# A gated cross-attention and expert layer on one core: block 4's GpSimd parts behind the context's low parts, and block 5's norm and turn inside a second layer

## The chip, the cores and the metric

The kernel runs on one core of a Trainium2 chip (trn2). The metric is the device time of one execution in microseconds; the median of three runs counts. Engines are called TensorE (PE in the profile), VectorE (DVE), ScalarE (ACT), GpSimd (POOL) and SyncE (SP). SyncE only issues DMA transfers here.

## The reference

The input x has 16 sequences of 256 rows of 256 numbers, the context 16 sequences of 120 rows. Cut to what matters:

```python
# cross part: z is the context, x the normalized input
z  = z @ W_in + b_in
zn = layernorm(z)
h  = silu(pe @ Wp1 + bp1) @ Wp2 + bp2            # taps, times a decaying window
c  = (causal convolution of zn with window * h, every second row)
xr = ffn(x)                                      # layernorm, W1a, silu, W1b, + x
y  = ffn(xr * c)                                 # layernorm, W2a, silu, W2b, + x
x  = x + tanh(g_xattn) * y
# expert part: 8 heads of 32 numbers, 16 experts, the best 2 of each row and head
t  = (layernorm(x) @ Wm + bm), rows and heads as rows
w  = softmax(t @ expert_emb), top 2
out = sum over the two of w * (gelu(t @ W1[e] + b1[e]) @ W2[e] + b2[e])
x  = x + tanh(g_ffn) * (out @ Wo + bo)
```

## The kernel before, in words

The 4096 rows of x are 8 blocks of 512 rows. Each engine has its program written out by hand, in one order, and waits on semaphores that count finished steps. Numbers that need more precision than 16 bits are split in a high and a low 16-bit part, and a product is three matmuls: high by high, high by low, low by high.

The first stage goes over the blocks with s = 1 to 8. For block s, TensorE does the second layer of block s-1 (`layer2`, L650: bias, then 4 quarters k of 12 products) and the first layer of block s (`layer1`, L633), with the input turned by TensorE (`turn`, L604, eight transposes) from the normalized block. The norm itself is VectorE's: `first_norm(b)` takes the statistics (L973, L980, L1012, L1013), GpSimd raises to the power -1/2 (`power`, L1713), and `normed_twice(b)` writes the normalized rows (L990; on ScalarE for blocks 3 and 4). ScalarE writes the high part of the turned input (L1523), VectorE the low part (`turn_lo`, L956). After the first layer ScalarE writes the activation twice, as a high part and in full (L1529, L1534), and GpSimd subtracts the two for the low part (`layer1_lo`, L1719). `first_out(b)` on VectorE (L1155) ends the block.

The context is normalized in pieces in the gaps (`context_part`, L1118, L1121). At s = 4 ScalarE copies its high parts (`context_hi`, L1618) and VectorE subtracts the low parts (`context_lo`, L1131) in five pieces; semaphore `v_zl` counts them.

The convolution has 32 chunks of 8 channels. A chunk is 32 small matmuls (`conv`, L676), ScalarE's copy of the sums (`conv_sums`, L1546), TensorE's turn back (`flip`, L696, four or so transposes, one chunk behind) and VectorE's addition (`conv_out`, L1139), counted by `v_dc`; `flip(c)` waits for the output of chunk c-2. Chunks 0 to 7 follow the first layer of block 4, 8 to 15 that of block 5, 16 to 23 that of block 6, and 24 to 31 come at s = 7. So blocks 5, 6 and 7 are turned inside the convolution, ahead of chunks 6, 14 and 22 (`turn_ahead`), into PSUM banks that nothing else uses then.

The taps of a chunk (four DMA transfers of 134 KB, `load_T`, L386) go in a ring of ten places. SyncE issues those of chunk c+10 or so when chunk c is done. Its queue also holds the swaps of the context's halves (`swap_context`, L441) and the loads of x (`load_x`, L374): block 7's x goes to the place of block 5's, so it waits for block 5's norm (`v_nm` at 6). When the convolution is done, the gating, the second feed-forward layer and the expert part follow; nothing of them is changed.

ScalarE splits the weights of the later stages at s = 5 (L1514, L1516), and VectorE takes their low parts then (L940).

Of the kernel before, what the change touches and what calls it, by code (L numbers as in the profile page):

```python
# [13 lines left out]
NB = 8  # L14
NC = 32
# [50 lines left out]
def turn3(b):  # L66
    return norm3(b)
# [15 lines left out]

def turn_ahead(c):

    return c // 8 + 5 if c % 8 == 6 and c < NC - 8 else None


AGAIN = (4, 5, 6, 8, 9, 0, 1, 2)
# [55 lines left out]
def flamingo_kernel(nc, xd, ctxT, peT, wp1, wp2, win, w1a, w1b, w2a, w2b, wm, wo,  # L145
                    ew1, ew2, eb, cols, rows, ident, ramp, tvec, ones, out):
    with ExitStack() as ctx:
# [11 lines left out]
        W1 = {h: sb("W1" + h, 2048, F16) for h in "hl"}  # L159
# [210 lines left out]
        def sync_program(sp):  # L370
# [73 lines left out]
            for s in range(1, NB + 1):  # L444
                if s in (2, 4):
                    sp.wait_ge(v_nm, s + 1)
                    load_x(0, 5 if s == 2 else 6)
                if s == 4:
                    swap_context(0)
                    swap_context(1)  # L450
                for c in chunks(s):
                    for e in next_in_place(c):
                        load_T(e)
                    if c < 3:
                        swap_context(c + 2)
                    if c == 3:
                        sp.wait_ge(v_nm, 6)
                        load_x(0, 7)
                if s == NB - 1:
                    for b in range(2):  # L460
                        sp.wait_ge(v_nm, 8 - b)
                        load_x(1, b)
# [75 lines left out]
        def tensor_program(pe):  # L538
# [98 lines left out]
            def layer2(j, w, halfway=None):  # L637

                o = [PB[:, 256 * t:256 * t + 256] for t in range(4)]
                bias = BR[:, 256 * (j // NB):256 * (j // NB) + 256].unsqueeze(1).broadcast_to([128, 2, 256])  # L640
                for h in range(2):
                    pe.matmul(PB[:, 512 * h:512 * h + 512].rearrange("p (t n) -> p t n", t=2), ON[:, 0:128], bias,
                              start=True, stop=False)
                for k in range(4):
                    if k == 2 and halfway:
                        halfway()
                    pe.wait_ge(g_slo, 4 * j + k + 1)
                    for t in range(4):
                        for a, b in THREE:
                            m = pe.matmul(o[t], S[b][:, 512 * k + 128 * t:512 * k + 128 * t + 128],  # L650
                                          w[a][:, 1024 + 256 * k:1024 + 256 * k + 256],
                                          start=False, stop=(k == 3 and t % 2 == 1 and a + b == THREE[2]))
                m.then_inc(p_l2, 1)
# [59 lines left out]
            def first_gated():  # L713
                gated_turn(0)

            def third_turn(b):
                pe.wait_ge(*((a_n3, b + 1) if b < 7 else (v_n3, 1)))
                turn(turn3(b), WSP[:, 1024 * b:1024 * b + 1024])
# [52 lines left out]
            for s in range(1, NB + 1):  # L771
                if s < 5:
                    first_turn(s)
                if s == 3:
                    pe.wait_ge(l_w2, 80)
                    pe.wait_ge(a_silu, 11)
                    affine_bias(1, PA[:, 1024:1152])
                if chunks(s - 1):
                    pe.wait_ge(v_dc, UPTO[s - 1] - 1)
                if s == 1:  # L780
                    pe.wait_ge(v_w1l, 3)
                    pe.wait_ge(v_tap, 2)
                    pe.wait_ge(g_br, 1)
                    pe.wait_ge(g_one, 1)
                else:
                    pe.wait_ge(v_out, s - 1)
                layer2(s - 1, W1, first_gated if s == NB else None)
                if s == 7:
                    convs(s)
                if s < NB:  # L790
                    layer1(s, s, W1)
                if s < 7:
                    convs(s)
# [143 lines left out]
        def vector_program(ve):  # L937
# [77 lines left out]
            def normed_twice(b):  # L1015
                o = 160 + 48 * (b % 3)
                ve.wait_ge(g_pow, b + 1)
                if b == 2:
                    ve.wait_ge(g_br, 1)
                apply(x_place(b)[0], XN0[b % 3], SM[:, o + 24:o + 32], SM[:, o + 36:o + 40], v_nm)  # L1020
# [8 lines left out]
            def once_over_twice(b):  # L1029

                o = 160 + 48 * (b % 3)
                ve.reciprocal(SM[:, o + 40:o + 44], SM[:, o + 36:o + 40]).then_inc(v_rc, 1)
                ve.wait_ge(v_rc, b + 1)
                ve.scalar_tensor_tensor(out=SM[:, o + 40:o + 44], in0=SM[:, o + 40:o + 44], scalar=SC,
                                        in1=SM[:, o + 32:o + 36], op0=ALU.mult, op1=ALU.mult).then_inc(v_rho, 1)
# [284 lines left out]
            once_over_twice(2)  # L1320
            first_norm(3)
            for s in range(2, NB):
                if s < 5:
                    turn_lo(s)
                if s == 3:
                    layer1_bias(1, PA[:, 1024:1152])
                if s < 5:
                    context_part(*CTX[s][0])
                if s < 4:
                    twice_shift(s + 1)  # L1330
                    once_over_twice(s + 1)
                elif 4 < s < NB - 1:
                    normed_twice(s + 1)
                    once_over_twice(s + 1)
                if s < 5:
                    context_part(*CTX[s][1])
                if s == 5:
                    ve.wait_ge(a_wm, 1)
                    split_lo(WMS, WM["h"][:, :], WM["l"][:, :], v_wm)
                    ve.wait_ge(a_wo, 1)  # L1340
                    split_lo(WOS, WO["h"][:, :], WO["l"][:, :], v_wo)
                    for i, (c0, c1, scale) in enumerate(((0, 512, G2S[0]), (512, 1024, G2S[1]), (1024, 2048, SC))):
                        ve.wait_ge(a_w2h, i + 1)
                        split_lo(XR[:, 4096 + c0:4096 + c1], W2["h"][:, c0:c1], W2["l"][:, c0:c1], v_w2l, scale)
                if s == 6:
                    ve.wait_ge(a_eb, 1)
                    split_lo(EBF, EB["h"][:, :], EB["l"][:, :], v_eb)
                if s == 4:
                    context_lo(0)
                first_out(s - 1)  # L1350
                if s == 4:
                    for u in range(1, 5):
                        context_lo(u)
                elif s + 2 < NB:
                    first_norm(s + 2)
                if s < 5:
                    context_part(*CTX[s][2])
                for c in chunks(s):
                    if c % 8:
                        conv_out(c - 1)  # L1360
                    if turn_ahead(c):
                        turn_lo(turn_ahead(c))
                    if c == 2:
                        normed_twice(5)
                        once_over_twice(5)
                    if c == 4:
                        first_norm(6)
                    if last(c):
                        conv_out(c)
            gate(0)  # L1370
# [139 lines left out]
        def scalar_program(ac):  # L1510
# [121 lines left out]
                        layer1_full(s, C_B1A, 3)  # L1632

            for s in range(1, NB):
                if s < 5:
                    turn(s)
                if s in (2, 3):
                    normed_twice(s + 1)
                if s == 5:
                    ac.wait_ge(l_w2, 80)  # L1640
                    split_hi(WMS, WM["h"][:, :], a_wm)
                    split_hi(WOS, WO["h"][:, :], a_wo)
                    for k in range(2):
                        split_hi(XR[:, 4096 + 512 * k:4608 + 512 * k], W2["h"][:, 512 * k:512 * k + 512], a_w2h, G2S[k])
                    split_hi(XR[:, 5120:6144], W2["h"][:, 1024:2048], a_w2h)
                if s == 6:
                    split_hi(EBF, EB["h"][:, :], a_eb)
                if s == 7:
                    convs_summed(s)
                if s == 4:  # L1650
                    for u in range(3):
                        context_hi(u)
                    for n in range(2):
                        layer1(s, C_B1A, (n,))
                        context_hi(n + 3)
                else:
                    layer1(s, C_B1A, range(3 if s in (5, 6) else 4))
                if s < 7:
                    convs_summed(s)
# [48 lines left out]
        def pool_program(po_):  # L1708
# [35 lines left out]
            po_.wait_ge(v_zep, 1)  # L1744
            po_.tensor_tensor(zr, zr, SM[:, 6:7].broadcast_to([128, 16]), ALU.pow).then_inc(g_zpow, 1)
            for s in range(1, NB - 1):
                layer1_lo(s)
                if s + 2 < NB:
                    power(s + 2)
# [123 lines left out]
```

## Time and profile before

| what | value |
|---|---|
| median of 3 runs | 797.74 us (796.12 to 798.57) |
| the profiled execution | 796.66 us |
| its span, first to last instruction | 794.9 us |
| mean granted TensorE clock | 0.998 |
| TensorE busy | 765.6 us, 96% |
| VectorE busy | 564.6 us, 71% |
| ScalarE busy | 662.9 us, 83% |
| GpSimd busy | 506.2 us, 64% |

The profile is of one execution. A stage is read from the rows of its own stretch, since the shares are means over stages that differ. "issue" as a releaser is time in which an engine waited for nothing that the profile shows. The DMA share is a mean over the core's 16 DMA engines and can come out somewhat over 1. A clock of 1 is 2.4 GHz, of 0.5 it is 1.2 GHz.

### The profile page before, as it was taken

To read this page: it belongs to the slowest core of one execution; us is meant where nothing else is said; L and a number is where in the kernel's file an instruction comes from. 1 tells how busy PE (TensorE), PEld (TensorE's weight loads), DVE (VectorE), ACT (ScalarE), POOL (GpSimd) and SP (SyncE) were. 2 spreads that over 40 slices of the span, in tenths; PEclk is the share of its full clock that TensorE was granted. 3 is DMA by queue.
4 is the path that set the end of the run, shared out by engine and by line. 5 is a ranking of instruction groups with operands and counts; after the bars stand their busy time and mean duration, and the time that the engine had idled before them with its cause. 6 is when DMAs were issued, how large, how long until landed. Compare 5 with 4: busy or idle time off the path is not lost.

```text
span 794.9 us, 23935 instructions
## 1 busy us (share of the span) xinstructions
PE 765.6 (96%) x9972; PEld 384.9 (48%) x9972; DVE 564.6 (71%) x1031; ACT 662.9 (83%) x837; POOL 506.2 (64%) x389
## 2 busy tenths in 40 slices
PE   9999789889899999999999999999999999999997
PEld 4667456655576664333344444444444434444433
DVE  5998963478788995675776776776776776775445
ACT  4464844367778867799999999999999999999995
POOL 1365331047764452587788788787797787797674
PEclk9999999999999999999999999999999999999999
DMA  8994599930123325757455555655555565555542
GB/s 292 222 234 91 127 198 196 204 91 27 34 77 91 75 66 141 173 150 191 140 162 153 162 150 160 170 148 162 159 158 157 154 171 150 158 163 152 168 148 68
DMA packets 86122, 117.07 MB, mean 147 GB/s; under 512 B 13154, under 2 KB 65746, under 8 KB 85915
## 3 DMA queue, kind: packets, MB, share of 16 engines
q1 hardware_dynamic: 86014, 115.55, 55.8%
q8 instruction: 78, 1.28, 0.7%
q14 instruction: 30, 0.24, 0.1%
HBM read 101.28 MB, written 6.94 MB: 136 GB/s over the span
## 4 chain that ended last, share of the span: by engine, by line
PE 76%; DVE 11%; ACT 6%; issue 4%; POOL 3%; POOLq 0%; DVEq 0%; ACTq 0%
PE PB L851 26%; PE PA L839 18%; PE PT L839 9%; PE PB L650 5%; PE PA L633 5%; PE PB L873 2%; DVE WK L956 2%; PE PA L585 2%; ACT WK L1694 2%; DVE SM L973 2%; ACT WK L1559 1%; POOL WK L1719 1%; PE PT L731 1%; DVE DC L1139 1%; PE PB L696 1%
## 5 line engine op out<-in xcount | busy, mean ns | idle before, releaser
L1786 POOL TENSOR_TENSOR WK<-WK 128x512 f32<-128x512 f32 x238 | 330.5, 1389 | 94.4 <-DVE WK L1418 83.9
L1694 ACT ACTIVATE WK<-PA 128x1024 f32<-128x1024 f32 x349 | 354.9, 1112 | 7.5 <-PE PA L839 7.5
L851 PE MATMUL PB<-WK,EW 128*32 128x512 f32 x2040 | 264.8, 593 | 0.3 <-DVE WK L1418 0.3
L839 PE MATMUL PA<-RA,EW 98*32 98x512 f16 x2800 | 200.7, 378 | 1.6 <-ACT WK L1694 1.6
L1694 ACT ACTIVATE WK<-PT 128x1024 f32<-128x1024 f32 x163 | 182.2, 1118 | 0.1
L1719 POOL TENSOR_TENSOR WK<-WK 128x512 f16<-128x512 f32 x64 | 83.5, 1316 | 124.0 <-ACT WK L1534 123.0
L839 PEld LDWEIGHTS PA<-RA,EW 98*32 98x32 f16 x2800 | 71.7, 95 | 149.6 <-issue 78.7
L839 PE MATMUL PT<-RA,EW 98*32 98x512 f16 (+1 forms) x1312 | 99.5, 378 | 0.3 <-ACT WK L1694 0.2
L851 PEld LDWEIGHTS PB<-WK,EW 128*32 128x32 f32 x2040 | 63.4, 111 | 50.7 <-DVE WK L1418 1.1
L1418 DVE SCALAR_TENSOR_TENSOR WK<-PB,CV,W2h 128x512 f32<-128x512 f32 x64 | 48.1, 751 | 42.0 <-PE PB L851 41.4
L1418 DVE SCALAR_TENSOR_TENSOR WK<-PB,CV,DC 128x512 f32<-128x512 f32 x64 | 48.1, 751 | 38.2 <-PE PB L851 37.3
L1418 DVE SCALAR_TENSOR_TENSOR WK<-PB,CV,W1h 128x512 f32<-128x512 f32 x64 | 48.0, 751 | 32.5 <-PE PB L851 29.2
L839 PEld LDWEIGHTS PT<-RA,EW 98*32 98x32 f16 x1312 | 34.3, 95 | 69.4 <-issue 37.2
L1418 DVE SCALAR_TENSOR_TENSOR WK<-PB,CV,W2l 128x512 f32<-128x512 f32 x63 | 47.3, 751 | 26.6 <-PE PB L851 25.7
L1529 ACT ACTIVATE WK<-PA,CV 128x512 f16<-128x512 f32 x64 | 44.2, 691 | 24.6 <-PE PA L633 24.0
L1713 POOL TENSOR_TENSOR SM<-SM 128x4 f32<-128x4 f32 (+1 forms) x24 | 33.2, 1385 | 39.7 <-DVE SM L986 22.7
L650 PE MATMUL PB<-W2h,WK 128*128 128x256 f16 x256 | 42.6, 273 | 4.5 <-POOL WK L1719 4.5
L1534 ACT ACTIVATE WK<-PA,CV 128x512 f32<-128x512 f32 x64 | 44.3, 692 | 0.0
L650 PE MATMUL PB<-W1h,WK 128*128 128x256 f16 x256 | 42.4, 273 | 0.0
L633 PE MATMUL PA<-WK,W1h 128*128 128x512 f16 x128 | 38.1, 379 | 0.0
L633 PE MATMUL PA<-WK,W2h 128*128 128x512 f16 x128 | 38.1, 379 | 0.0
L650 PE MATMUL PB<-W2l,WK 128*128 128x256 f16 x128 | 34.9, 273 | 0.0
(238 smaller groups left out, 1090.9 us busy)
## 6 DMA issues: line engine op xcount, KB each, us to landing
W1h<-wtd SPq DMA_DIRECT2D x128, 128.0 KB, 2.7
DC<-wtd SPq DMA_DIRECT2D x128, 128.0 KB, 2.8
W2h<-wtd SPq DMA_DIRECT2D x128, 128.0 KB, 2.8
W2l<-wtd SPq DMA_DIRECT2D x128, 128.0 KB, 2.8
RA<-wpd SPq DMA_DIRECT2D x96, 134.1 KB, 5.7
WK<-in_x SPq DMA_DIRECT2D x15, 512.0 KB, 4.1
RA<-DC SPq DMA_DIRECT2D x96, 64.0 KB, 2.0
out<-WK SPq DMA_DIRECT2D x16, 256.0 KB, 2.8
```

What stands on the lines that cost most here:

```text
L585: a = pe.matmul(PA[64 * r:64 * r + 64, 512 * q0 + 256 * b:512 * q0 + 256 * b + 256], DC[:, 2048 * k + 128 * bb + 64 * r:2048 * k + 128 * b ...
L633: m = pe.matmul(pa, w[a][:, 512 * k + 128 * n:512 * k + 128 * n + 128], xt[b][:, 512 * k:512 * k + 512], start=(i == 0), stop=(i == 5))
L650: m = pe.matmul(o[t], S[b][:, 512 * k + 128 * t:512 * k + 128 * t + 128], w[a][:, 1024 + 256 * k:1024 + 256 * k + 256], start=False, stop= ...
L839: m = pe.matmul(pre(k)[32 * j:32 * j + 32, w * q:w * q + w], EW1[0:98, 128 * e + 32 * j:128 * e + 32 * j + 32], TS[0:98, h, t0:t0 + w], st ...
L851: m = pe.matmul(o[32 * q:32 * q + 32, :], EW2[:, 32 * e:32 * e + 32], hb[:, 512 * q:512 * q + 512], start=True, stop=True)
L1418: ve.scalar_tensor_tensor(out=dst, in0=po("down", n), scalar=col(C_B2 + e), in1=WB[n // 2 % 4][:, 512 * (n % 2):512 * (n % 2) + 512], op0= ...
L1529: ac.activation(S["h"][:, 512 * n:512 * n + 512], PA[:, 512 * n:512 * n + 512], ACT.Silu, scale=1.0 / SC, bias=col(bcol + n))
L1534: ac.activation(SF[n], PA[:, 512 * n:512 * n + 512], ACT.Silu, scale=1.0 / SC, bias=col(bcol + n)).then_inc(a_silu, 1)
L1694: ac.activation(HB[n % NH][:, 1024 * p:1024 * p + 1024], pre(k)[:, :], ACT.Gelu, scale=1.0 / (SC * SC)).then_inc(a_gelu, 1)
L1713: po_.tensor_tensor(SM[:, o:o + n], SM[:, o:o + n], SM[:, 6:7].broadcast_to([128, n]), ALU.pow).then_inc(g_pow, 1)
L1719: po_.tensor_tensor(sl, SF[n], sh, ALU.subtract).then_inc(g_slo, 1)
L1786: po_.tensor_tensor(AC[g], AC[g], PR[m % 3], ALU.add).then_inc(g_ac, 1)
```

## The change

Four things are moved. GpSimd's four parts of block 4's first layer now wait until all five low parts of the context are done. VectorE's `normed_twice` and `once_over_twice` of block 5 and `first_norm` of block 6, which stood in the convolution's chunks 2 and 4, come after chunk 7, with the low part of block 5's turn behind them; `normed_twice` and `once_over_twice` of block 6 move behind the output of block 4. Block 5's turn leaves the convolution (chunk 6) and stands between the second and the third quarter of block 4's second layer on TensorE, and before the weight splits on ScalarE. SyncE's load of block 7's x moves from chunk 3 to chunk 5.

```diff
--- before.py
+++ after.py
@@ -83,7 +83,7 @@
 
 def turn_ahead(c):
 
-    return c // 8 + 5 if c % 8 == 6 and c < NC - 8 else None
+    return c // 8 + 5 if c in (14, 22) else None
 
 
 AGAIN = (4, 5, 6, 8, 9, 0, 1, 2)
@@ -453,7 +453,7 @@
                         load_T(e)
                     if c < 3:
                         swap_context(c + 2)
-                    if c == 3:
+                    if c == 5:
                         sp.wait_ge(v_nm, 6)
                         load_x(0, 7)
                 if s == NB - 1:
@@ -712,6 +712,9 @@
 
             def first_gated():
                 gated_turn(0)
+
+            def fifth_turn():
+                first_turn(5)
 
             def third_turn(b):
                 pe.wait_ge(*((a_n3, b + 1) if b < 7 else (v_n3, 1)))
@@ -784,7 +787,7 @@
                     pe.wait_ge(g_one, 1)
                 else:
                     pe.wait_ge(v_out, s - 1)
-                layer2(s - 1, W1, first_gated if s == NB else None)
+                layer2(s - 1, W1, {5: fifth_turn, NB: first_gated}.get(s))
                 if s == 7:
                     convs(s)
                 if s < NB:
@@ -1320,7 +1323,11 @@
             once_over_twice(2)
             first_norm(3)
             for s in range(2, NB):
-                if s < 5:
+                if s == 5:
+                    normed_twice(5)
+                    once_over_twice(5)
+                    first_norm(6)
+                if s < 6:
                     turn_lo(s)
                 if s == 3:
                     layer1_bias(1, PA[:, 1024:1152])
@@ -1329,9 +1336,9 @@
                 if s < 4:
                     twice_shift(s + 1)
                     once_over_twice(s + 1)
-                elif 4 < s < NB - 1:
-                    normed_twice(s + 1)
-                    once_over_twice(s + 1)
+                elif s == 6:
+                    normed_twice(7)
+                    once_over_twice(7)
                 if s < 5:
                     context_part(*CTX[s][1])
                 if s == 5:
@@ -1352,6 +1359,9 @@
                     for u in range(1, 5):
                         context_lo(u)
                 elif s + 2 < NB:
+                    if s == 5:
+                        normed_twice(6)
+                        once_over_twice(6)
                     first_norm(s + 2)
                 if s < 5:
                     context_part(*CTX[s][2])
@@ -1360,11 +1370,6 @@
                         conv_out(c - 1)
                     if turn_ahead(c):
                         turn_lo(turn_ahead(c))
-                    if c == 2:
-                        normed_twice(5)
-                        once_over_twice(5)
-                    if c == 4:
-                        first_norm(6)
                     if last(c):
                         conv_out(c)
             gate(0)
@@ -1632,7 +1637,7 @@
                         layer1_full(s, C_B1A, 3)
 
             for s in range(1, NB):
-                if s < 5:
+                if s < 6:
                     turn(s)
                 if s in (2, 3):
                     normed_twice(s + 1)
@@ -1744,6 +1749,8 @@
             po_.wait_ge(v_zep, 1)
             po_.tensor_tensor(zr, zr, SM[:, 6:7].broadcast_to([128, 16]), ALU.pow).then_inc(g_zpow, 1)
             for s in range(1, NB - 1):
+                if s == 4:
+                    po_.wait_ge(v_zl, 5)
                 layer1_lo(s)
                 if s + 2 < NB:
                     power(s + 2)
```

## Rows read from the trace of the kernel before

**Rows 1.** The page: the profiled span.

```profile
span 794.9 us, 23935 instructions
```

**Rows 2.** Windows: busy us of PE, PEld, DVE, ACT, POOL; clock; DMA; GB/s.

```profile
118.60:122.80 4.20, 4.15 (x76) 3.08 (x75) 0.69 (x1) 1.79 (x3) 0.00 (x0) 0.60 1.11 192
104.00:158.00 54.00, 46.83 (x845) 31.59 (x843) 23.63 (x51) 22.59 (x40) 10.87 (x9) 0.97 1.11 201
```

**Rows 3.** The chain that ended last: start us, us, what.

```profile
98.42 0.61 PE PB L642 x2
...
104.27 5.18 PE PA L633 x24
...
115.10 3.56 issue
...
142.73 0.87 issue
...
161.51 1.24 issue
```

**Rows 4.** Timeline of DVE: start us, us, engine, line, operation, out<-in [idle before <-releaser].

```profile
82.35 6.02 DVE L1131 TENSOR_TENSOR RA<-DC,RA 128x512 f16<-128x512 f32 x4
...
89.68 2.22 DVE L990 TENSOR_SCALAR WK<-WK,SM 128x256 f32<-128x256 f32 x4
...
94.72 0.38 DVE L980 BATCH_NORM_AGGREGATE SM<-SM 128x2 f32<-128x6 f32 x4
...
98.87 1.38 DVE L990 TENSOR_SCALAR RA<-WK,SM 128x256 f32<-128x256 f32 x4
...
102.98 1.22 DVE L940 SCALAR_TENSOR_TENSOR W2l<-XR,W2h 128x1024 f16<-128x1024 f32 x1
...
106.36 1.41 DVE L973 BATCH_NORM_STATS2 SM<-WK 128x6 f32<-128x256 f32 x4 [0.30 <-DMA WK<-in_x]
```

**Rows 5.** Line L1131, 78 to 90 us: duration ns min/median/max, starts, forms.

```profile
L1131 DVE TENSOR_TENSOR RA<-DC,RA x5: 685/1214/2180, 80.2 to 87.2; 128x1024 f16<-128x1024 f32 x3, 128x512 f16<-128x512 f32 x2
```

**Rows 6.** Timeline of PE, 89 to 114 us.

```profile
89.22 0.66 PE L696 MATMUL PB<-ID,RMP 128*128 128x128 f32 x4 [0.45 <-DVE DC L1139]
...
92.84 0.66 PE L696 MATMUL PB<-ID,RMP 128*128 128x128 f32 x4 [1.25 <-DVE DC L1139]
93.33 1.04 PE L604 MATMUL PA<-ID,WK 128*128 128x128 f32 x8
...
113.09 0.65 PE L696 MATMUL PB<-ID,RMP 128*128 128x128 f32 x4
```

**Rows 7.** Timeline of POOL: the first and the last of four.

```profile
82.84 1.21 POOL L1719 TENSOR_TENSOR WK<-WK 128x512 f16<-128x512 f32 x1 [7.02 <-ACT WK L1534]
...
90.14 1.28 POOL L1719 TENSOR_TENSOR WK<-WK 128x512 f16<-128x512 f32 x1 [0.76 <-ACT WK L1534]
```

**Rows 8.** Timeline of ACT: the first and the last of the weight splits.

```profile
96.64 0.62 ACT L1514 ACTIVATE WMh<-WK 128x512 f16<-128x512 f32 x1
...
98.90 1.05 ACT L1514 ACTIVATE W2h<-XR 128x1024 f16<-128x1024 f32 x1
```

**Rows 9.** Timeline of SP's DMA issues.

```profile
98.89 2.69 SPq L386 DMA_DIRECT2D RA<-wpd  x4
101.63 0.42 SPq L374 DMA_DIRECT2D WK<-in_x  x1
102.09 6.69 SPq L386 DMA_DIRECT2D RA<-wpd  x12
```

**Rows 10.** Landing us of the x load issued at 101.63; the page's DMA issues.

```profile
DMA to landing us min/median/max: 4.7/4.7/4.7
...
XR<-in_w1b SPq DMA_DIRECT2D x1, 512.0 KB, 11.4
```

**Rows 11.** DMA queues, 99.8 to 115.6, 115.6 to 118: packets, MB, share.

```profile
q1 hardware_dynamic: 5292, 3.15, 101.8%
...
q8 instruction: 1, 0.02, 3.4%
```

## The prediction

> **What bounds the kernel now.** I read the page first, then the chain of work that ended last, then each engine's timeline from 80 to 126 us, where the edits lie. The profiled execution took 796.66 us for a span of 794.9 [rows 1], 1.8 outside it; the median of the three runs is 797.74, so I make the sum on the profile and add 1.1. The edits touch only what lies between 80 and 166 us, the end of the convolution, so a gain has to come from there and survive to 166.
>
> In that stretch three things set the pace. Up to 98.4 it is VectorE: its low parts of the context, one group of 6.02 us [rows 4], and then a norm of 2.22 us and the statistics, with TensorE waiting 0.45 and 1.25 us for a convolution output [rows 6]. From 98.42 TensorE runs the second layer of block 4 (to 104.27, 5.85 us with its wait) and the first layer of block 5 without a pause [rows 3]. From 104 to 158 the DMA engines are full, at a share of 1.11 and 201 GB/s [rows 2], with tap loads. There the chain has three pauses called "issue", of 3.56, 0.87 and 1.24 us [rows 3]. They wait for no semaphore. Over 99.8 to 115.6 us, 5292 packets of the data queue moved and none of an instruction queue; in the next 2.4 us one packet of the instruction queue came [rows 11], and TensorE went on at 118.65, the end of the 3.56 us pause. So I read them as TensorE out of code, because its next block of instructions stood behind full data queues. After that pause the granted clock is 0.60 over 118.6 to 122.8 [rows 2], which is mostly the lower of the two levels, 1.2 GHz, and costs 4.2 x 0.4 = 1.7 us.
>
> **GpSimd waits for the context's low parts.** Five VectorE subtractions of 0.69 (small) or 1.21 (large) us took up to 2.18 when a GpSimd part of 1.21 us ran beside them [rows 5, 7]. Two are slowed, so 2 x 0.97 = 1.9 us leave the group of 6.02; the last one cannot begin before ScalarE's high part, so I count 1.3. The Trainium skill (SBUF — State Buffer, Who interferes with whom) says a VectorE instruction with two SBUF inputs blocks against a GpSimd one that reads SBUF, and a reduction never does; the trace agrees on the first by 2.18 against 1.21. GpSimd's four parts of some 1.3 us each then end near 92.3 instead of 91.4 [rows 7]; layer 2 of block 4 needs them after 94.8, so that costs nothing. If the cover went, the price would be at most that 0.9.
>
> **The norms and the turn leave the convolution of block 4.** Out of it go, on VectorE, the norm (2.22, of which 0.84 is contention, since its twin takes 1.38 [rows 4]), its reciprocal, the statistics (1.4 plus 0.6 of small ones) and the turn's low part (1.3); on TensorE, the turn, 1.04 [rows 6]. TensorE then goes at the pace of a convolution and a flip, 1.15 us a chunk (my estimate: from the flip at 113.09 [rows 6] to the pause at 115.10 [rows 3], in which lie two flips, one convolution and the first instruction of chunk 13, are 2.0 us, so 1.7 without that instruction for one and a half chunks). The flip at 89.22 loses its wait of 0.45 and comes near 88.7; from there this gives chunk 7 at 92.75, its flip at 94.1, and layer 2 of block 4 at 94.8: 3.6 us earlier than 98.42.
>
> Inside layer 2 the turn comes after the bias and half the products, some 3.1 of its 5.85 us, at 97.9. It needs block 5's norm: VectorE finishes the last two outputs at 95.4, and 1.38 more is 96.8. One microsecond to spare, so no wait; a norm slowed once by GpSimd (0.84) still fits. The turn puts 1.0 us back, and layer 1 of block 5 begins at 94.8 + 5.85 + 1.0 = 101.6, 2.6 us before 104.27. Its operand's low part is done at 100.5. ScalarE does its high part by 99.6 (my estimate: the end of the turn at 98.9 and half a microsecond) and only then the weight splits, which took from 96.64 to 99.95, 3.3 us [rows 8]: to 102.9, just when layer 1 asks for its first activation (101.6 and a quarter of its 5.18 us). Free, with nothing to spare. VectorE's own splits follow ScalarE's and end with one of 1.22 [rows 4], at 104.3, so the output of block 4 ends at 106.0, much as before. The convolution of block 5 would begin at 106.8 instead of 109.4.
>
> **What is late next: the last x block.** VectorE now does the norm of block 6 after that output (1.4, or up to 3.1 if GpSimd hits two of its four pieces), to 107.4 to 109.1, and then wants the statistics of block 7. On SyncE's queue the load of that x moves from behind chunk 3's tap load to behind chunk 5's, past eight DMA issues, and gains a wait for block 5's norm (96.8, long fulfilled). Queued behind it are the tap loads of chunks 16 on, wanted at 137, so nobody feels them. The load went out at 101.63 and landed 4.7 us later [rows 9, 10], at 106.3, when VectorE had waited 0.30 for it [rows 4]. Twelve issues take 6.69 us [rows 9], so eight take some 4: it goes out at 105.5 to 106.1. Below, with the same 4.7 us, it lands at 110.2. Above, by bytes: two tap loads of four DMAs of 134 KB are 1.07 MB now ahead of it, at 201 GB/s 5.4 us, so 111.7. I take 111.7, because the DMA engines are full. Then statistics 2.0, output of chunk 8 0.7: 114.4. The flip of chunk 10, which waits for that output and was at 113.09 [rows 6], comes at 114.5: TensorE stands idle 4 us (113.09 - 2.6 = 110.5, to 114.5). The convolution of chunk 13 follows 1.7 later, at 116.2. Before, it got its first instruction in and then the rest at 118.65, the end of the pause. Its code block is asked for some 2.6 us sooner and should be there by about 115.5. So the pause of 3.56 is replaced by this wait of 4, the lower clock after it stays, and the gain at this point is 118.65 - 116.2 = 2.4 us.
>
> **How much of it is left at 166.** TensorE now asks for each later block 2.4 us sooner, but the data queues empty no sooner: the DMA engines are busy to 158 with the same bytes [rows 2]. Two code pauses lie ahead, at 142.7 and 161.5 [rows 3]. If a block comes after all the data queued before it, TensorE gets it at the old hour; if its delay is fixed, it moves with the request. I take the middle, half kept: 1.2 us. Sum: 796.66 - 1.2 = 795.5 on the profile, 796.6 beside the median. From -0.3 to +0.3% is about what a measurement of this kernel cannot tell from no change; that is 2.4 us. The convolution's end is followed by VectorE's gate and then fixed work, so what is left at 166 is left at the end.
>
> The skill has two rules on this. Runtime: NRT & Kernel Launch (Instruction fetch mechanics) holds that refills are mostly hidden; the trace disagrees, by the 3.56 us pause; were it so, chunk 13 would not have paused before, and the wait for x would make the change 1.4 us slower there (114.5 against 113.09). DMA: Bandwidth & Descriptors (Queues, rings and completion order) says each DMA engine goes round its queues packet by packet; then a block's delay would not hang on the depth of the data queue, and the sum would be the "kept" rival's.
>
> **Rivals.**
> - Code blocks fully bound to the data stream: TensorE comes to the pause before 161.5 earlier and leaves it at the same 162.75. Gain 0: 797.7. For it: the DMA share of 1.11 that stays to 158. Against: the later pauses are short.
> - Kept: the delay moves with the request, all 2.4 us stay: 795.3. For it: the two later pauses are no longer than 1.24, though the queues are as full. Against: the pause of 3.56.
> - More than that: x lands at 110.2, or the 4 us idle does not lower the clock (1.7 us back). Then 2.4 + 1.5 or + 1.7, about 4.0: 793.7. Against: 3.56 us of idle did lower it.
> - Slower: the x load comes late. The longest landing of a 512 KB load is 11.4 us [rows 10]; from 105.5 it would be at 116.9, chunk 13 at 121.4, later than 118.65 by 2.8: 800.5. It decides from a landing past 114.1 (loss), and past 116.5 for 0.3%. Against: that one stood behind a row of large loads.
> - The change does nothing where it is put: the turn halfway waits for the norm and gives back the 2.6. It needs VectorE 1.1 us late before it costs anything, and 3.7 to cost all; it ends at 797.7 too, and I count it with the first rival.
>
> **Chances.** Forecast (half kept) 0.38; bound to the stream 0.22; kept 0.15; more 0.14; slower 0.11. Faster by over 0.3%: 0.14 and two thirds of the kept case (it lies on the border), 0.24. Slower: 0.11. Within: 0.65. The range has to reach both sides: 793.7 leaves out the far half of the "more" case, 799.3 nearly all of the slower one. The forecast's own range is 795.3 to 797.7.
>
> **What would show it.** No VectorE low part over 1.25 us; layer 2 of block 4 at 94.8 and layer 1 of block 5 at 101.6; a turn between its products without a wait; the wait of VectorE for x up from 0.3 to 2.5 to 4 us; a TensorE wait of 4 us for VectorE ahead of chunk 10's flip, and no "issue" pause at chunk 13; then "issue" pauses before chunks 21 and 29 longer than 0.87 and 1.24 by one to two microseconds together. It is wrong if the x load lands by 109, if chunk 13 still pauses for code, if the clock stays at 2.4 GHz, or if ScalarE's splits make layer 1's first activation late.

## The result, and the profile after

The changed kernel takes 798.87 us (median of 22 runs, 797.45 to 800.93), the kernel before 797.31 (22 runs, 792.28 to 801.47). The ratio is 1.0025, with a 95% interval of 1.0013 to 1.0037: slower by 0.25%, some 2 us (1.6 us between the medians): clear of the noise, though small. The forecast was 796.6, faster by 0.15%. The profiled execution of the changed kernel took 800.92 us, which is the slow end of its runs; a second profile, of an execution of 798.82, is read beside it below.

The chain of work that ended last, in the changed kernel (start us, us, what; SPq is SyncE's queue of DMA issues):

```profile
101.70 0.43 SPq L386
...
104.74 0.67 SPq L386
105.41 0.04 issue
105.45 9.34 DMA WK<-in_x
114.79 0.02 issue
114.81 1.42 DVE SM L976 x4
...
116.91 0.60 DVE DC L1142
117.51 0.04 issue
117.55 1.11 PE PB L696 x4
...
149.38 0.60 PE PB L642 x2
...
161.48 2.53 issue
164.01 0.90 PE PA L696 x3
...
169.87 0.70 DVE DC L1142
```

The same chain in the kernel before, where the last pause of [rows 3] lies between its two rows:

```profile
149.40 0.61 PE PB L642 x2
...
166.49 0.70 DVE DC L1139
```

The timelines of TensorE and VectorE in the changed kernel:

```profile
94.43 0.60 PE L642 MATMUL PB<-BR,ON 128*128 128x512 f16 x2
97.49 1.04 PE L604 MATMUL PA<-ID,WK 128*128 128x128 f32 x8
100.98 0.59 PE L633 MATMUL PA<-WK,W1h 128*128 128x512 f16 x2
...
109.41 0.63 PE L676 MATMUL PA<-RA 60*32 60x256 f16 x32
117.55 0.69 PE L696 MATMUL PB<-ID,RMP 128*128 128x128 f32 x2 [7.52 <-DVE DC L1142]
...
120.62 1.05 PE L676 MATMUL PA<-RA 60*32 60x256 f16 x32
```

```profile
105.48 2.88 DVE L993 TENSOR_SCALAR RA<-WK,SM 128x256 f32<-128x256 f32 x4
...
114.81 1.41 DVE L976 BATCH_NORM_STATS2 SM<-WK 128x6 f32<-128x256 f32 x4 [6.16 <-DMA WK<-in_x]
```

The same kernel in windows; the columns are those of [rows 2]:

```profile
112.00:122.20 10.20, 4.65 (x75) 2.93 (x76) 4.60 (x14) 1.04 (x2) 1.63 (x1) 0.50 1.12 185
163.20:170.00 6.80, 5.99 (x80) 3.84 (x81) 2.21 (x4) 1.19 (x2) 0.00 (x0) 0.50 0.16 30
```

And the kernel before behind its last pause:

```profile
161.50:168.00 6.50, 5.03 (x88) 3.12 (x88) 3.12 (x5) 1.83 (x4) 0.00 (x0) 1.00 0.28 78
```

What is to be seen. Up to the convolution of block 5 the change does what it was to do: layer 2 of block 4 starts at 94.43 instead of 98.42, and layer 1 of block 5 at 100.98. Then the chain no longer runs through TensorE but through SyncE's queue: the x load of block 7 goes out at 105.45, behind the tap loads, and lands 9.34 us later. VectorE waits 6.16 us for it where it waited 0.30 [rows 4], and TensorE waits 7.52 us for VectorE's output, longer than the 3.56 us pause for code that is gone [rows 3]. The clock is at its lower level from 112.0, inside that wait, to 122.2; TensorE is busy for 4.65 of these 10.2 us. The convolution of chunk 13, which had its first instruction at 114.82 and the others at 118.65 before, starts at 120.62, and layer 2 of block 5 at 127.15 instead of 126.04. Even so layer 2 of block 6 starts at 149.38, as in the kernel before (149.40 in its chain): the pause of 0.87 us at 142.7 is gone too. The loss comes behind it. The last pause begins at the same time as before (161.48, before 161.51) but grows from 1.24 to 2.53 us, and the clock falls at its end, at 163.2, for 6.8 us, in which TensorE is busy for 5.99. The last output of the convolution starts at 169.87 instead of 166.49.

The clock is not a matter of one profile: the 22 executions of the changed kernel had a mean granted clock of 0.988 to 0.994 (median 0.991), 99 executions of the kernel before, on the chips of the experiments, 0.990 to 1.000 (median 0.996). Half a per cent of the time is 4 us of full speed; part of it fell into waits, so the 4 us are an upper estimate of its price.

### The profile page after: what moved, and what is told of

Its sections match the earlier page's. It is cut to its first block, busy times and chain, and to the rows that moved or that the text cites. A ratio compares the mean times of both kernels' runs of the same rounds, so it can differ in the third digit from the quotient of the medians.

```text
span 799.1 us, 23936 instructions
## 1 busy us (share of the span) xinstructions
PE 767.9 (96%) x9972; PEld 395.0 (49%) x9972; DVE 563.1 (70%) x1031; ACT 662.8 (83%) x837; POOL 506.2 (63%) x389
## 3 DMA queue, kind: packets, MB, share of 16 engines
q8 instruction: 78, 1.28, 0.7%
## 4 chain that ended last, share of the span: by engine, by line
PE 72%; DVE 9%; ACT 7%; SPq 4%; issue 3%; POOL 3%; DMA 2%; POOLq 0%; DVEq 0%; ACTq 0%
PE PB L854 26%; PE PA L842 18%; PE PT L842 9%; PE PB L650 4%; PE PA L633 4%; PE PB L876 2%; PE PA L585 2%; SPq L386 2%; DVE WK L959 2%; ACT WK L1699 2%; DVE SM L976 2%; ACT WK L1564 1%; DMA WK<-in_x 1%; POOL WK L1724 1%; ACT WK L1539 1%
## 5 line engine op out<-in xcount | busy, mean ns | idle before, releaser
L842 PEld LDWEIGHTS PA<-RA,EW 98*32 98x32 f16 x2800 | 75.3, 95 | 146.2 <-issue 75.0
L854 PEld LDWEIGHTS PB<-WK,EW 128*32 128x32 f32 x2040 | 66.6, 111 | 48.3 <-DVE WK L1423 1.9
L842 PEld LDWEIGHTS PT<-RA,EW 98*32 98x32 f16 x1312 | 36.0, 95 | 67.8 <-issue 35.5
```

The source lines that it names most:

```text
L842: m = pe.matmul(pre(k)[32 * j:32 * j + 32, w * q:w * q + w], EW1[0:98, 128 * e + 32 * j:128 * e + 32 * j + 32], TS[0:98, h, t0:t0 + w], st ...
L854: m = pe.matmul(o[32 * q:32 * q + 32, :], EW2[:, 32 * e:32 * e + 32], hb[:, 512 * q:512 * q + 512], start=True, stop=True)
```

## The experiments

All ratios are against the kernel before, run on the same chip, with 95% intervals; the chips differ from one group of experiments to the next. A profile is of one execution, and executions of one kernel differ by up to 10 us, so times from two profiles are weaker evidence than the ratios. In every profile of the study, the span less the start of the last convolution output is 628.3 to 629.2 us, so the difference between kernels lies nearly all ahead of that output.

**The x load back behind chunk 3** (in the changed kernel):

```diff
-                    if c == 5:
+                    if c == 3:
                         sp.wait_ge(v_nm, 6)
                         load_x(0, 7)
```

> The changed kernel, with SyncE's load of block 7's x back behind chunk 3's tap load. Theory (the moved load is what costs): the load goes out at 101.2 us and lands near 106, VectorE waits at most 1 us for it, TensorE's wait of 7.8 us before the flip of chunk 10 falls to 1 to 1.5 us, the granted clock does not fall at 112, and the kernel is 2 to 5 us faster than the changed one: 794 to 797. Rival (the moved load only fills a pause that would come anyway, TensorE waits for code instead): a pause of 3 us or more marked issue comes near chunk 13, and the time stays within 1 us of the changed kernel, near 799.

Measured: 795.04 us, 0.9972 [0.9945, 0.9999]; the changed kernel's ratio is 1.0025. The load landed after 5.2 us, VectorE did not wait for it, and TensorE's wait fell to 1.28. TensorE in that kernel:

```profile
109.72 0.63 PE L676 MATMUL PA<-RA 60*32 60x256 f16 x32
111.63 0.66 PE L696 MATMUL PB<-ID,RMP 128*128 128x128 f32 x4 [1.28 <-DVE DC L1142]
...
113.36 0.28 PE L676 MATMUL PA<-RA 60*32 60x256 f16 x1
114.94 0.30 PE L676 MATMUL PA<-RA 60*32 60x256 f16 x8 [1.30 <-issue]
```

The theory holds: the load's new place costs the kernel some 0.5%, more than the whole loss, and with the load in its old place the rest of the change gains about what was forecast. The last pause did not go: it is 2.64 us in this profile, again with a low clock behind it. The profiled execution (797.25 us) is one of the slower ones of this kernel; its executions took 790.47 us (mean clock 1.000) to 799.57 us (0.993), so the pauses do not come in all of them at this length.

**Only the x load moved** (in the kernel before, the reverse edit alone).

> The kernel before, with only that load moved from behind chunk 3's to behind chunk 5's tap load. Theory (the load's hour alone costs): it goes out near 105.5 and lands near 115, VectorE waits 8 us for it, the flip of chunk 10 comes near 117.5 instead of 113.1, and the kernel is 1.5 to 4 us slower than before. Rival (the loss comes from the moved norms and turn): at most 0.5 us slower, because the pause for code at chunk 13 covers it.

Measured: 797.97 us, 1.0008 [0.9993, 1.0024]. Landing 7.3 us, VectorE's wait 6.44, but TensorE's only 2.08, for here it is ready for the flip some 2.5 us later than in the changed kernel, and no pause for code at chunk 13 follows. The theory's 1.5 to 4 us did not come. So the rival holds for this edit alone: the late load is covered by a stall that was there. It seems to cost only where the other edits have brought TensorE forward.

The two kernels side by side show where a lead ends. First the x load alone, then the changed kernel with the load behind chunk 3 (end of block 6's chunks, the last pause, the last output):

```profile
148.73 0.61 DVE DC L1139
...
165.14 0.70 DVE DC L1139
```

```profile
146.92 0.61 DVE DC L1142
...
159.68 2.64 issue
...
167.00 0.70 DVE DC L1142
```

The second is 1.8 us ahead at chunk 23 and 1.9 us behind at chunk 31. It reaches the border of its code block early, waits 2.64 us, and then runs at 1.2 GHz:

```profile
163.80:167.20 3.40, 3.40 (x44) 2.19 (x43) 1.59 (x3) 0.90 (x2) 0.00 (x0) 0.50 0.29 65
```

The first comes late, finds its block there and keeps its clock from chunk 23 on (it had lost it before, for 3.4 us from 142.2, at a pause of 1.62).

**The second layer's x loads behind the convolution.** SyncE issues two loads of 512 KB at 152 to 155 us, ahead of TensorE's last code block. In this edit they are issued after `p_conv` has counted all chunks:

```diff
-                if s == NB - 1:
-                    for b in range(2):
-                        sp.wait_ge(v_nm, 8 - b)
-                        load_x(1, b)
             sp.wait_ge(p_conv, NC)
             sp.dma_start(ES[0:98, :], ew1).then_inc(l_ew, 16)
+            for b in range(2):
+                sp.wait_ge(v_nm, 8 - b)
+                load_x(1, b)
```

In the changed kernel:

> The changed kernel, with the two loads of x for the second layer (SyncE, at 152 us in the kernel before) moved behind the end of the convolution. Theory (TensorE's code blocks come only when the data issued before them has drained, and the last pause of the convolution is set by these 1 MB): the pause of 2.5 us at 161.5 and the low clock after it are gone or under 1.5 us, the convolution ends near 166 instead of 169.9, and the kernel is 2 to 4 us faster than the changed one: 795 to 797. Rival (the pause is of another kind, or the block's delay is fixed): pause and time as in the changed kernel, 799.

In the kernel before:

> The kernel before with the same two loads moved behind the end of the convolution. Theory: the pause of 1.24 us at 161.5 shrinks to under 0.5 us, 0.8 to 2 us faster than before: 795.5 to 796.7. The pause at chunk 13 (3.56 us) stays, since those loads come later. Rival: no change, 797.5; or slower, because the second layer now waits for x.

Measured: 794.10 us, 0.9972 [0.9949, 0.9995], and 794.20 us, 0.9956 [0.9936, 0.9975]. In both profiles the last pause is gone, and the clock is at 2.4 GHz from 121.1 us on at the latest. The changed kernel with this edit, from chunk 23 to 31:

```profile
146.71 0.61 DVE DC L1141
...
162.99 0.70 DVE DC L1141
```

16.3 us where the changed kernel took 21.1 (148.72 to 169.87), although its own wait for the x of block 7 is still there (TensorE 4.02 us). Both gains are above or at the upper end of what was expected (the second was to be 0.8 to 2 us; it is 2.5 us between the medians and 3.5 by the ratio). The executions say where it comes from: the kernel before took 791.93 to 800.96 us on that chip, with the edit 791.74 to 795.74. The fastest are no faster; the slow ones are gone. So in many executions the pause with its clock seems to cost the kernel before more than in the profiled one.

The instruction queue shows the block itself. Its packet lies in the half microsecond from 160.0 in the kernel before, from 161.5 in the changed one, and from 156.5 and 155.5 in the same two with the x loads moved (packets, MB, share of the 16 engines):

```profile
q8 instruction: 1, 0.02, 14.0%
q8 instruction: 1, 0.02, 13.8%
q8 instruction: 1, 0.02, 17.8%
q8 instruction: 1, 0.02, 12.7%
```

| us | x loads issued | border before the last passed | packet of the last block | TensorE past the border | pause |
|---|---|---|---|---|---|
| before | 152.3 | 157.3 | 160.4 | 162.8 | 1.24 |
| only the x load of block 7 moved | 151.9 | 157.3 | 159.0 | 161.4 | none |
| changed | 155.3 | 157.3 | 161.6 | 164.0 | 2.53 |
| changed, x behind chunk 3 | 153.3 | 155.5 | 159.8 | 162.3 | 2.64 |
| before, x loads behind the convolution | 162.8 | 156.1 | 156.6 | 160.0 | none |
| changed, x loads behind the convolution | 162.0 | 155.3 | 155.8 | 159.2 | none |

In all thirteen profiles a pause for code from 108 us on ends 2.4 to 3.1 us after its packet, so the packet sets its end. In the nine with the x loads in front, that packet comes between 159.0 and 161.6, whether TensorE passed the border before it at 155.1 or at 157.3, and it is latest (161.6) where these loads were issued latest (155.3). In the two versions without them it comes 0.5 us after that border is passed.

**Code blocks shifted.** In the kernel before, 48 small matmuls stand at TensorE's start, 96 records, into a bank that is overwritten before use.

```diff
             pe.wait_ge(g_one, 1)
+            for _ in range(48):
+                pe.matmul(PT[0:32, 0:32], ON[:, 0:32], ON[:, 0:32], start=True, stop=True)
             ones(6)
```

> The kernel before with 48 matmuls of 32 columns more at TensorE's start, 96 instruction records, written to a bank that is overwritten before use. Theory (the pauses marked issue stand at the borders of code blocks of 256 instructions): each of the pauses at the records 2240, 3008 and 3777 comes 96 records of the old program earlier, so the one at chunk 13 moves to about chunk 11 or 12 and the one of chunk 29 to chunk 27 or 28, and the old places run through. The time is within 1.5 us of before plus up to 2 us for the matmuls. Rival (the pauses belong to those instructions, or to a moment of the data stream): they stay at the same chunks.

Measured: 796.03 us, 0.9994 [0.9970, 1.0019]. The profiled execution is the slowest of its twelve (802.38). The windows count TensorE's records from the start to the begin of each long pause. The kernel before, then the shifted one:

```profile
0.00:115.10 115.10, 108.65 (x1095) 67.64 (x1096) 95.99 (x261) 65.90 (x106) 48.14 (x42) 1.00 0.83 194
0.00:142.70 142.70, 131.51 (x1469) 83.08 (x1470) 105.86 (x282) 76.74 (x125) 52.83 (x46) 0.99 0.88 194
0.00:161.50 161.50, 148.26 (x1843) 95.45 (x1843) 114.60 (x296) 82.63 (x136) 52.83 (x46) 0.99 0.90 195
```

```profile
0.00:119.20 119.20, 112.17 (x1221) 71.36 (x1222) 96.93 (x262) 67.90 (x110) 48.09 (x42) 1.00 0.85 193
0.00:145.10 145.10, 134.97 (x1595) 86.53 (x1595) 106.94 (x284) 78.86 (x129) 52.72 (x46) 0.99 0.89 192
0.00:159.20 159.20, 147.24 (x1844) 95.49 (x1845) 113.58 (x295) 81.85 (x134) 52.72 (x46) 0.99 0.91 191
```

Matmuls and weight loads together are 2191, 2939 and 3686 before, and 2443, 3190 and 3689 shifted. With TensorE's semaphore instructions, which the trace has and the windows leave out, the counts are 2241, 3009 and 3777, and 2497, 3265 and 3777: all apart by multiples of 256. The shifted program has a shorter pause of 0.61 us at 113.60 too, behind record 2241. In all thirteen profiles every "issue" pause of 0.6 us or more between 108 us and the convolution's end stands behind record 2241, 2497, 3009, 3265 or 3777. So the pauses sit at fixed counts of the instruction stream and not at a chunk: the theory holds. The expectation that all three come 96 records earlier in the program was right for the last and, as the 0.61 us, for the first; two long ones stand one block further on, for which borders pause depends on when TensorE gets there and when the packet comes. The shifted program's last pause is 4.72 us, the longest of the study.

The Trainium skill (Runtime: NRT & Kernel Launch, Instruction fetch mechanics) gives refills of 256 instructions; the trace agrees, by these counts. It also says the cost of a border is mostly hidden; the trace agrees for six of the seven borders that the changed kernel's profile passes between 110 and 165 us, and not for the ones with pauses of 2.5 to 4.7 us.

**Both corrections together** (the changed kernel, x of block 7 behind chunk 3, the second layer's x behind the convolution).

> The changed kernel with block 7's x load back behind chunk 3 and the two x loads of the second layer behind the end of the convolution. Theory: both prices of the change are gone: no wait of VectorE for x over 1 us, no pause over 1.5 us at the last code block and no low clock after it; the convolution ends near 163.5 and the kernel takes 791 to 793.5, faster than both. Rival (something else holds the end of the convolution): 795, as with the first of the two edits alone.

Measured: 792.04 us, 0.9939 [0.9919, 0.9959]: faster than both kernels, by 0.6% than the one before. The convolution's last outputs start at 160.49, better than the 163.5 expected, and what bounds it in this profile is a tap load at last:

```profile
152.29 5.92 DMA RA<-wpd
158.22 0.14 issue
158.35 1.05 PE PA L675 x27
```

Most of the lead of this profile was there before the moved loads' turn came: chunk 23's output starts at 141.42, against 146.92 with the first correction alone, and the pause behind record 3009 is 0.34 us instead of 2.17. The second correction changes nothing ahead of it, so that part belongs to the execution; for the kernels, the ratios count.

**GpSimd's wait.** Alone in the kernel before, and taken out of the changed kernel:

```diff
             for s in range(1, NB - 1):
+                if s == 4:
+                    po_.wait_ge(v_zl, 5)
                 layer1_lo(s)
```

> The kernel before with only GpSimd's wait for the context's five low parts. Theory: no low part over 1.25 us, the norm of block 5 at 1.4 to 3.1 us (GpSimd now runs beside it), layer 2 of block 4 at most 1.3 us earlier, and nothing left of it at the end of the convolution: within 1 us of before. Rival: all 1.3 us stay, 796.

> The changed kernel without GpSimd's wait. Theory: layer 2 of block 4 begins 1.3 us later than in the changed kernel (95.9 instead of 94.6), the x load still goes out near 105.5 and lands near 115, so nothing changes behind it: within 1 us of the changed kernel, near 799. Rival (GpSimd's wait itself costs, by parts that come late): 1 us or more faster than the changed kernel.

Measured: 796.47 us, 0.9995 [0.9977, 1.0014], and 797.65 us, 1.0009 [0.9993, 1.0025]. Then out of the two corrected versions:

> The changed kernel with block 7's x load back behind chunk 3 and without GpSimd's wait: only the norms and the turn are moved. Theory (the norms and the turn give the gain, GpSimd's wait adds at most 1.3 us at the start of layer 2 of block 4, which the code pauses swallow): as with the load moved back and the wait in place, 0.997 of before within 0.15%. Rival (GpSimd's wait gives a good part of the gain): 0.999 to 1.000 of before.

> The fastest version so far (block 7's x load behind chunk 3, the second layer's two x loads behind the convolution) without GpSimd's wait. Theory: its end of the convolution is bound by the tap load of chunk 31, so the wait is worth nothing there: 0.994 of before within 0.15%. Rival: the wait's 1.3 us count in full, 0.9955.

Measured: 795.93 us, 0.9990 [0.9967, 1.0012] (0.9972 with the wait), and 793.36 us, 0.9946 [0.9927, 0.9965] (0.9939 with it). The four comparisons differ in sign, none is over 0.2%, and their intervals overlap; which way the wait works stays open. Not all came as expected. With the wait alone, layer 2 of block 4 began at 99.42, not earlier than 98.42. The changed kernel without it was to take some 799 us with x landing near 115; it took 797.65, with a landing at 111.9. The version with x behind chunk 3 was to be within 0.15% of 0.997 without the wait; 0.9990 fits the rival, that the wait gives a good part of the gain. The last version hit its number, but in its profile no tap load bounds the end, which comes at 158.03. The wait does shorten the low parts (at most 1.23 us with it, 2.18 without); a gain from that at the end is not shown.

**The changed kernel once more.**

> The changed kernel once more, for a second profile. Theory (the x load lands 7.2 to 9.3 us after its issue, as in four profiles with the moved load): TensorE waits 3.5 to 8 us before the flip of chunk 10, at least one pause for code or a low clock is gone or new against the first profile, and the time is 0 to 0.4% above the kernel before. Rival (the landing of 9.3 us belongs to that one execution): 7.2 to 7.6 again, a wait under 4.5 us, and the time as with the moved load and without GpSimd's wait, within 0.1% of before.

Measured: 797.61 us, 1.0013 [0.9994, 1.0033], as the theory had it. The load landed after 8.6 us, at 112.5, TensorE waited 4.52, chunk 13 started at 118.34, and both low stretches are there again:

```profile
113.90:120.70 6.80, 5.43 (x79) 3.71 (x80) 3.45 (x12) 1.19 (x2) 1.64 (x1) 0.50 1.12 188
161.70:168.50 6.80, 5.95 (x80) 3.84 (x81) 2.18 (x4) 1.19 (x2) 0.00 (x0) 0.50 0.14 31
```

So the second stretch does not hang on the 7.52 us wait of the first profile. TensorE comes to the last border at 159.57, 1.9 us before the kernel before, and pauses 2.97 us; it leaves at 162.54, 0.2 before it. The last output starts at 168.40, 1.9 us behind it.

## Why the prediction was wrong, point by point

**What failed first: the lead at chunk 13.** The sum had the x load landing at 111.7, the flip of chunk 10 at 114.5, and chunk 13 at 116.2, 2.4 us ahead of 118.65. It landed at 114.8, the flip came at 117.55 and chunk 13 at 120.62, 2.0 behind; in the second profile at 112.5, 115.27 and 118.34, 0.3 ahead. Of the 4.4 us in the first profile, 3.1 are the landing. The other 1.4 are the clock: the prediction kept the low clock but took 1.7 us from the flip to chunk 13 from rows at full clock, while the clock fell inside the wait and that way took 3.07 us in both profiles.

The landing was 106.3 plus 5.4, from 1.07 MB at 201 GB/s. The issue at 105.45 was right in the first profile (105.5 to 106.1 was forecast) and came at 103.9 to 104.7 in the four others with the load behind chunk 5. There the landing takes 7.2 to 9.3 us; with the load behind chunk 3 it takes 4.7 to 7.1 in eight profiles, so the 4.7 it was built on is the shortest of a spread. What shares the rate with the load was not settled. TensorE waited 7.52 and 4.52 us, not 4.0. The prediction's slower rival named this mechanism and its point ("past 114.1") but gave it 0.11. Undoing it is worth 0.5%: with the load behind chunk 3 the ratio is 0.9972. It is still not the whole loss in the first profile, for at 149.38 the changed kernel was level with the one before.

**What failed next: how much of a lead is left at 166.** The prediction took "the middle, half kept: 1.2 us", between keeping all and keeping nothing, as if a TensorE that comes early to a code border could only wait there until "the old hour". The runs show a third answer, below the lower bound: the pause can end later than before, and the clock falls in it. In the second profile a lead of 1.9 us at the last border left 0.2 behind it. In the first there was no lead at that border, and the block itself came 1.2 us later (161.6 against 160.4), as the x loads in front of it had been issued 3.0 us later. The last pause was 2.53 and 2.97 us in the two profiles, against 1.24, and in it the granted clock fell to 0.50 for 6.8 us, where the kernel before kept 1.00. 5.95 to 5.99 us of busy time at half clock is some 3 us of work lost. The experiments isolate it: with nothing but the 1 MB of x loads taken from in front of the last code block, both the pause and the low clock go, and the ratio of the changed kernel falls from 1.0025 to 0.9972. That the clock falls because of the longer pause is argued, from the order in the profiles: in all six with a last pause of 2.5 us or more a low stretch begins in it or behind it, and in the six with 1.24, 0.38 or none there is none. The combined version had a pause of 0.51 there and several short waits for tap loads, and its clock fell at 157.1 for 3.4 us, so a single long pause is not the only way to it; and at chunk 13 a pause of 2.55 us left the clock at 1.00 in the kernel before with the x loads moved, so it is not a sure one either.

**What held.** The largest low part took 1.23 us (no more than 1.25 was forecast). Layer 2 of block 4 came at 94.43 (94.8), layer 1 of block 5 at 100.98 (101.6), the turn inside the second layer at 97.49 (97.9) without a wait. The norm of block 6, hit by GpSimd, took 2.88 us (1.4 to 3.1), hidden by the wait for x. The pause for code at chunk 13 was replaced by the wait for VectorE; its block's packet came at 111.2 and 112.0 in the two profiles instead of 115.7, in time as forecast. The low clock stayed, but with 4.65 us of busy time in it instead of 3.4. "Pauses longer before chunks 21 and 29" was half right: the one at 142.7 went, the other grew by 1.3.

**The rivals.** "Bound to the data stream" was the right mechanism at the last border, as read from [rows 11], with the wrong floor. The Trainium skill (DMA: Bandwidth & Descriptors, Queues, rings and completion order) has the engines go round their queues packet by packet; from this the "kept" rival had all of the lead stay. The last block's packet does not bear it out: it came 1.7 to 6.2 us after TensorE passed the border before, in the nine profiles with the x loads in front, where one data packet took 0.06 to 0.07 us, and 0.5 to 2.4 us after it in the four without them. How the engines chose between the queues was not tested.

## What to carry to other kernels

A pause marked "issue" on an engine with a long unrolled program is a late code block when its count of records from the start stays fixed while the program shifts under it. Data issued ahead of it on full DMA queues made it late here, so a large load that nobody needs yet is worth holding back until the engine has crossed the next border; that was worth 0.44% here, where the change with its x load in the old place gave 0.28% at its best. And a lead won ahead of such a border is not a gain: ask how long the engine will stand there and whether the clock falls, and when a load is moved past others on a full queue, price it by the longest landing seen in that stretch, not by its bytes or by the landing of one profile.

## What the runs showed of the hardware

The load of block 7's x, 512 KB, took 4.7 to 9.3 us to land, depending on place and execution, with the DMA engines at a share of 1.1. TensorE's pauses without a releaser stood behind records 2241, 2497, 3009, 3265 and 3777 of its stream, 256 or a multiple apart, and ended 2.4 to 3.1 us after a packet of 16 KB on the instruction queue; one such packet came for each 256 records, and only after the border before had been passed. TensorE's clock fell to 0.50 in stretches of 3.4, 6.8 and 10.2 us; in two profiles a single wait of 4.02 and 4.52 us had 6.8 us of it, which began some 0.4 and 1.4 us before TensorE went on. The kernel before varied from 792.28 to 801.47 over 22 runs; that this is the convolution's end moving is likely (158.0 to 172.1 us over the profiles of the study, with some 628.5 us behind it in each), though only one execution of that kernel was profiled.
